# Sums of exponentials over edges of one source, as matmuls on a rounded part and a rest

## The chip, the cores and the metric

The kernel runs on one core of a Trainium2 chip. The metric is the device time of one execution in microseconds. Three runs of the kernel before gave a median of 1133.86 us (1133.8 to 1134.31).

## The reference

Four graph layers work in turn on a state of 16 batches, 512 nodes and 128 features: a diffusion layer, a graph attention layer ("gat"), an edge attention layer ("edge") and a Chebyshev layer with self-attention and a feed-forward part ("cheb", "att", "ffn"). The change lies in the edge layer alone. With E = 256 edges and 4 heads it is, per batch:

```
Qs = Xq[:, src];  Kt = Xq[:, dst]
e = einsum('behd,hd->beh', leaky_relu(Qs + Kt, 0.2), a)
e = e + log(A0[src, dst] + 1e-08)
m = segment_max(e_t, src)
ex = exp(e_t - m[src])
denom = segment_sum(ex, src)
attn = ex / denom[src]
Y = segment_sum(attn * Vt, src)
```

So each edge and head has an exponential, and these are summed over all edges with the same source. All is in f32.

## The kernel before

Every batch goes through the layers alone, and different batches are in different layers at the same time. A front part (up to about 410 us) computes the diffusion layer for all batches and, squeezed into it, the gat and edge layers of the first batches. Then each engine works through a list of steps, written out by hand. A fill list (FILL_ORDER) comes first, then ten rounds of one fixed list (ORDER), from 605 to 1037 us, then a drain list (DRAIN_ORDER). In a round the gat layer is at batch n, the edge layer at n - 1, the cheb layer at n - 2, attention at n - 3. A "+" behind a step's name in the list takes it from a batch further back. An engine does its steps strictly in the order of its list; between engines there are semaphores, which count, and `ready(engine, name, n, count, per)` waits until the semaphore has reached n x per + count.

Of the edge layer these steps matter here. Edges lie on the 128 partitions in ET = 2 groups; the small numbers of an edge (4 heads x 2 groups = 8 per partition) are rows of the tile edge_small.
- edge_le (VectorE, line 304): logit less the maximum.
- edge_exp (ScalarE, 263): the exponentials, into row 2 of edge_small.
- edge_den (TensorE, 374): the sums. The stationary matrix is a 128 x 128 block of same_src, which holds 1 where two edges have one source, and the moving part is the 4 exponentials of a group; 2 x 2 such matmuls, all in f32, go into the PSUM bank b0.
- edge_rden, edge_attn (VectorE, 309 and 313): the reciprocal of the sums, straight from b0, and the normalised weight.
- edge_u (VectorE, 318), edge_scatter (TensorE, 381): weighted values, and their sum over a node's edges.

In a round's list on VectorE the two attention masks att_mask12 and att_mask13 (line 2457) and the statistics n3_stats of the feed-forward part (line 2142) stand between edge_le and edge_rden. On TensorE edge_den follows edge_v (367), the values of an edge; behind edge_den come att_turn10 (2665), gat_pv0 (567), att_turn11 and edge_scatter.

Elsewhere in the kernel, tiles of the type float32r ("R32") hold rounded f32 numbers, and products that need more accuracy are done on a rounded part and a rest, as in `for i, part in enumerate([h2_hi, h2_lo])` of edge_gather.

Of the kernel before, what the change touches and what calls it, by code (L numbers as in the profile page):

```python
# [61 lines left out]
def build(nc, t_in, out):  # L62
    ctx = ExitStack()
    with ctx:
        def sb(name, shape, dt=F32, c=None):
# [42 lines left out]
        same_src = sb("same_src", [P, ET, E])  # L108
# [34 lines left out]
        k["pair_words"] = 3 * NT * N + 4 * NT * D + 3 * E + ET * H * E // 2 + 6 * ET * H + ET * D + (6 + 2 + 4) * NT  # L143
# [52 lines left out]


def edge_stage(nc, k, sem):
# [73 lines left out]
    def on_vector(dve):  # L272
# [306 lines left out]
def build_front(nc, k):  # L579
# [3 lines left out]
    with ExitStack() as c:  # L583
# [469 lines left out]
        def _(dve):  # L1053
# [255 lines left out]
            def segments():  # L1309
                dve.wait_ge(sem("rows"), 2 * ET)  # L1310
                nc.vector.tensor_scalar(k.seg_bias[:], k.same_src[:], BIG, -BIG, ALU.mult, ALU.add
                                        ).then_inc(sem("seg"), 1)
# [4 lines left out]

            def with_layers(lev, t):
# [49 lines left out]
                elif (lev, t) == (2, 1):  # L1368
                    for h in range(H):
                        edge[f"edge_max{h}"](0)  # L1370
                    edge["edge_le"](0)
# [4 lines left out]
                    gat["gat_row3"](1)
                elif (lev, t) == (2, 2):
                    gat["gat_max0"](1)
                    gat["gat_max1"](1)
# [452 lines left out]
    "edge": """  # L1832
        edge_lc
# [44 lines left out]
        cheb_qlow edge_max0 edge_max1 edge_max2 edge_max3 edge_le att_mask12 att_mask13 n3_stats+ edge_rden edge_attn  # L1878
# [50 lines left out]
        gat_stats:3 edge_rden:1 edge_attn:1 edge_u:1 gat_aggr:3 att_mask0:0 att_mask1:0 edge_x3:1 cheb_stats:1  # L1929
        cheb_aggr:1 gat_apply:3 gat_x2a:2 gat_x2b:2 att_mask2:0 edge_stats:2 att_mask3:0 edge_aggr:2 att_mask4:0  # L1930
        att_mask5:0 cheb_lo:1 gat_scores0:3 gat_scores1:3 gat_scores2:3 gat_scores3:3 gat_row1:3 att_mask6:0
        gat_max0:3 gat_max1:3 gat_row2:3 gat_max2:3 gat_row3:3 cheb_y:1 att_mask7:0 n1_stats:1 att_mask8:0 n1_aggr:1
        edge_z:2 n1_apply:1 att_mask9:0 cheb_x1:1 edge_lc:2 gat_max3:3 att_mask10:0 edge_max0:2 edge_max1:2
        edge_max2:2 edge_max3:2 cheb_qlow:1 edge_le:2 att_mask11:0 att_mask12:0 gat_rinv:3 att_mask13:0 edge_rden:2
        edge_attn:2 edge_u:2 att_mask14:0 cheb_klow:1 att_mask15:0 gat_stats:4 att_rv:0 edge_x3:2 gat_aggr:4
        att_mask0:1 cheb_stats:2 gat_x2a:3 cheb_aggr:2 att_mask1:1 gat_x2b:3 edge_stats:3 att_mask2:1 edge_aggr:3
        gat_apply:4 att_scale:0 cheb_lo:2 att_mask3:1 ffn_y2:0 n2_stats:0 n2_aggr:0 att_mask4:1 n2_apply:0 att_mask5:1
        att_mask6:1 gat_scores0:4 gat_scores1:4 gat_scores2:4 gat_scores3:4 gat_row1:4 cheb_y:2 gat_row2:4 n1_stats:2
        att_mask7:1 n1_aggr:2 gat_row3:4 ffn_y3:0 gat_max0:4 gat_max1:4 gat_max2:4 att_mask8:1 att_mask9:1 n1_apply:2
        edge_z:3 gat_max3:4 cheb_x1:2 edge_lc:3 att_mask10:1 att_mask11:1 edge_max0:3 edge_max1:3 edge_max2:3  # L1940
        gat_rinv:4 edge_max3:3 edge_le:3 att_mask12:1 gat_stats:5 cheb_qlow:2 edge_rden:3 edge_attn:3 edge_u:3
        att_mask13:1 n3_stats:0 n3_aggr:0 gat_aggr:5 cheb_klow:2 att_mask14:1 n3_apply:0 att_mask15:1 edge_x3:3
        cheb_stats:3 att_rv:1 gat_x2a:4 gat_x2b:4 cheb_aggr:3 edge_stats:4 gat_apply:5 att_mask0:2 att_mask1:2
        edge_aggr:4 cheb_lo:3 att_scale:1 att_mask2:2 att_mask3:2 ffn_y2:1 n2_stats:1 att_mask4:2 n2_aggr:1
        att_mask5:2 n2_apply:1 att_mask6:2 cheb_y:3 n1_stats:3 gat_scores0:5 gat_scores1:5 gat_scores2:5 gat_scores3:5
        gat_row1:5 att_mask7:2 gat_row2:5 n1_aggr:3 ffn_y3:1 gat_row3:5 gat_max0:5 att_mask8:2 n1_apply:3 att_mask9:2
        gat_max1:5 cheb_x1:3 gat_max2:5 gat_max3:5 edge_z:4 edge_lc:4 att_mask10:2 att_mask11:2 edge_max0:4
        cheb_qlow:3 edge_max1:4 edge_max2:4 edge_max3:4 edge_le:4 att_mask12:2 att_mask13:2 n3_stats:1 edge_rden:4
        edge_attn:4
# [67 lines left out]
        att_mask15:13 edge_rden:15 edge_attn:15 edge_u:15 att_rv:13 n3_apply:12 att_mask0:14 edge_x3:15 cheb_stats:15  # L2017
        cheb_aggr:15 att_mask1:14 att_mask2:14 att_scale:13 att_mask3:14 cheb_lo:15 ffn_y2:13 n2_stats:13 n2_aggr:13
        att_mask4:14 n2_apply:13 cheb_y:15 n1_stats:15 n1_aggr:15 n1_apply:15 cheb_x1:15 att_mask5:14 att_mask6:14
        att_mask7:14 cheb_qlow:15 att_mask8:14 att_mask9:14 cheb_klow:15 att_mask10:14 att_mask11:14 att_mask12:14  # L2020
        att_mask13:14 ffn_y3:13 att_mask14:14 n3_stats:13 att_mask15:14 att_rv:14 n3_aggr:13 att_mask0:15 n3_apply:13
        att_mask1:15 att_mask2:15 att_scale:14 att_copy1:15 att_mask3:15 att_mask4:15 att_mask5:15 ffn_y2:14
        att_copy3:15 att_mask6:15 att_mask7:15 att_mask8:15 n2_stats:14 att_rv_0:15 att_copy5:15 n2_aggr:14
        att_mask9:15 att_mask10:15 n2_apply:14 att_copy7:15 att_mask11:15 att_mask12:15 att_copy9:15 att_mask13:15
        att_copy11:15 att_scale_0:15 att_mask14:15 att_mask15:15 att_copy13:15 ffn_y3:14 n3_stats:14 att_rv_1:15
        n3_aggr:14 ffn_y2_0:15 n2_stats_0:15 n2_aggr_0:15 att_copy15:15 n2_gain_0:15 n2_apply_0:15 n3_apply:14
        att_scale_1:15 ffn_y2_1:15 n2_stats_1:15 n2_aggr_1:15 n2_gain_1:15 n2_apply_1:15 ffn_y3_0:15 n3_stats_0:15
        n3_aggr_0:15 n3_gain_0:15 n3_apply_0:15 ffn_final_0:15 ffn_y3_1:15 n3_stats_1:15 n3_aggr_1:15 n3_gain_1:15
        n3_apply_1:15 ffn_final_1:15
# [771 lines left out]
```

## Time and profile before

| | |
|---|---|
| median of three runs | 1133.86 us |
| the profiled execution | 1133.88 us |
| its span | 1132.0 us |
| TensorE busy | 1083.0 us, 96% |
| VectorE busy | 853.7 us, 75% |
| ScalarE busy | 757.9 us, 67% |
| GpSimd busy | 344.9 us, 30% |
| mean granted TensorE clock | 0.989 |

All times are of one execution, in microseconds from the span's start. PE is the matmul part of TensorE, PEld its loading of stationary matrices, DVE is VectorE, ACT ScalarE, POOL GpSimd and SP the engine that issues transfers. A matmul of plain f32 leaves two records on PE, and two on PEld. What stands in brackets behind a row is the engine's idle time before it and what ended it. The granted clock is a share of the full 2.4 GHz.

### The profile page before, as it was taken

The page shows a single profiled execution, that of the slowest core. Times are in us where ns is not written, and L with a number is a line of the kernel's source. Part 1 is how long each engine was busy: PE and PEld are TensorE (multiplying, and loading weights), DVE is VectorE, ACT ScalarE, POOL GpSimd, SP SyncE. Part 2 cuts the span into 40 slices and gives each one's busy share as a digit, 9 for nine tenths or more (in the row PEclk, how much of TensorE's full clock was granted, in tenths as well). Part 3 has the DMA queues.
Part 4 walks back from the last instruction along what each step waited for, and adds up shares of the span by engine and source line. Part 5 has one row for each costly group of instructions (what it writes and reads, how often), then busy time and mean ns, then how long its engine had stood idle before and what let it go on. Part 6 is the DMA issues. An engine that isn't in the chain of part 4 may idle for free. (4 is left out here: it accounts for less than half of the span.)

```text
span 1132.0 us, 21408 instructions
## 1 busy us (share of the span) xinstructions
PE 1083.0 (96%) x7105; PEld 866.6 (77%) x7105; DVE 853.7 (75%) x3073; ACT 757.9 (67%) x1640; POOL 344.9 (30%) x465
## 2 busy tenths in 40 slices
PE   8999999999999978999999999999999999999876
PEld 5679889889889866777777877778778778777554
DVE  7774434444435558898999999999999999988766
ACT  4444434433313235988988988988988989988864
POOL 3302002301241112143253253253252352333333
PEclk9999999998999999999999999999999999999999
DMA  3002030030330112342352352343343443432531
GB/s 96 19 10 57 10 94 10 10 94 10 85 99 1 29 38 77 102 131 76 94 140 78 101 137 77 106 124 87 106 116 86 111 115 85 120 107 61 142 94 28
DMA packets 132941, 89.42 MB, mean 79 GB/s; under 512 B 13664, under 2 KB 115424, under 8 KB 132832
## 3 DMA queue, kind: packets, MB, share of 16 engines
q1 hardware_dynamic: 132768, 88.07, 28.3%
q8 instruction: 56, 0.92, 0.3%
q14 instruction: 53, 0.43, 0.1%
q0 software_dynamic: 64, 0.00, 0.0%
HBM read 33.50 MB, written 20.97 MB: 48 GB/s over the span
## 5 line engine op out<-in xcount | busy, mean ns | idle before, releaser
L2360 ACT ACTIVATE att_Es<-att_Ts,att_small 128x512 f32<-128x512 f32 x256 | 184.9, 724 | 8.9 <-DVE att_small L2457 8.2
L2457 DVE CUSTOM_DVE_ANT_0 att_Ts<-bank,mask_att 128x512 f32<-128x512 f32 x256 | 172.0, 683 | 22.4 <-PE bank L2612 18.3
L2369 ACT COPY att_PTs<-bank 128x512 f32<-128x512 f32 x248 | 144.5, 583 | 51.9 <-PE bank L2665 51.1
L2665 PE MATMUL bank<-ident,att_Es 128*128 128x128 f32 x1024 | 155.8, 275 | 6.8 <-ACT att_PTs L2369 6.6
L2665 PEld LDWEIGHTS bank<-ident,att_Es 128*128 128x128 f32 x1024 | 121.3, 142 | 42.8 <-ACT att_PTs L2369 17.3
L2612 PE MATMUL bank<-K_parts,Q_parts 128*128 128x512 f32 x256 | 113.1, 471 | 5.5 <-DVE att_small L2457 3.9
L2154 POOL TENSOR_SCALAR n_rs<-n_mv 128x4 f32<-128x4 f32 x46 | 15.5, 338 | 282.4 <-DVE n_mv L2149 282.4
L1597 PE MATMUL bank<-G_hi,UT_parts 128*128 128x384 f32 x288 | 79.1, 345 | 1.8 <-DVE G_lo L1440 1.8
L567 PE MATMUL bank<-gat_whs,gat_ETs 128*128 128x128 f32 x512 | 63.7, 280 | 2.0 <-PEq L149 2.0
L784 POOL TENSOR_SCALAR l_rs<-l_mv 128x4 f32<-128x4 f32 x16 | 3.8, 236 | 198.6 <-DVE l_mv L1064 198.2
L2612 PEld LDWEIGHTS bank<-K_parts,Q_parts 128*128 128x128 f32 x256 | 45.5, 190 | 24.2 <-issue 13.5
L567 PEld LDWEIGHTS bank<-gat_whs,gat_ETs 128*128 128x128 f32 x512 | 61.2, 196 | 2.4 <-issue 2.2
L1597 PEld LDWEIGHTS bank<-G_hi,UT_parts 128*128 128x128 f32 x288 | 54.0, 193 | 2.8 <-issue 2.2
L2733 PE MATMUL bank<-att_PTs,v_in 128*32 128x512 f32 x480 | 54.9, 593 | 0.4 <-ACT att_PTs L2369 0.4
L450 ACT ACTIVATE gat_Ts<-gat_Vs,gat_small 128x512 f32<-128x512 f32 x64 | 46.1, 722 | 7.9 <-DVE gat_Vs L505 7.6
L1603 PE MATMUL bank<-Z_hi,P3T_hi 128*128 128x512 f32 x128 | 51.2, 400 | 0.0
L1073 DVE TENSOR_TENSOR UT_parts<-bank,UT_parts 128x512 fp32r<-128x512 f32 x36 | 24.4, 687 | 34.9 <-ACT UT_parts L884 34.7
L1603 PE MATMUL bank<-Z_hi,P3T_lo 128*128 128x512 f32 x128 | 50.2, 393 | 0.0
L2360 ACT ACTIVATION_READ_ACCUMULATOR att_Es<-att_Ts,att_small 128x1 f32 x256 | 50.1, 196 | 0.0
L1603 PE MATMUL bank<-Z_lo,P3T_hi 128*128 128x512 f32 x128 | 49.8, 389 | 0.0
L1597 PE MATMUL bank<-G_lo,UT_parts 128*128 128x384 f32 x144 | 49.4, 343 | 0.0
L2156 POOL TENSOR_TENSOR n_rs<-n_rs,neg_half 128x4 f32<-128x4 f32 x46 | 47.8, 1040 | 3.8
(350 smaller groups left out, 2904.0 us busy)
## 6 DMA issues: line engine op xcount, KB each, us to landing
Q_parts<-q_hi SPq DMA_DIRECT2D x128, 64.0 KB, 2.2
Q_parts<-q_lo SPq DMA_DIRECT2D x128, 64.0 KB, 2.0
K_parts<-k_hi SPq DMA_DIRECT2D x128, 64.0 KB, 2.0
K_parts<-k_lo SPq DMA_DIRECT2D x128, 64.0 KB, 2.0
l_x<-in_x SPq DMA_DIRECT2D x16, 256.0 KB, 2.8
gat_z<-x_after_l SPq DMA_DIRECT2D x16, 256.0 KB, 3.3
gat_xin<-x_after_l SPq DMA_DIRECT2D x16, 256.0 KB, 3.7
attn_residual<-cheb_x1s SPq DMA_DIRECT2D x16, 256.0 KB, 2.2
```

The costliest lines, as they stand in the source:

```text
L450: nc.scalar.activation(g.T[:, t, :], g.V[:, t, :], ACT.Exp, scale=0.8, bias=small[:, 4, t:t + 1], accum_out=small[:, 6, t:t + 1]).then_inc ...
L567: mm = nc.tensor.matmul(a0[:, cols(t)], g.ET[:, s, cols(t)], WhA[:, s, 0:D], start=(s == 0), stop=(s == NT - 1))
L1073: nc.vector.tensor_tensor(UT[:, b % 2, i, 1, :], bank[[6, 4, 5][i]][:], UT[:, b % 2, i, 0, :].bitcast(F32), ALU.subtract).then_inc(sem("ut ...
L1597: mm = nc.tensor.matmul(bank[t][:, 0:BLOCKS * D], left, right[:, i, :], start=(i == 0 and p == 0), stop=(i == BLOCKS - 1 and p == 2))
L1603: mm = nc.tensor.matmul(bank[t][:], left[:, s, cols(t)], right[:, s, :], start=(first and i == 0), stop=(stop and i == 2))
L2156: nc.gpsimd.tensor_tensor(rs[:, 1, :], rs[:, 0, :], k.neg_half[:], ALU.pow).then_inc(sem(tag + "_rs"), 1)
L2360: nc.scalar.activation(att_E[:, j % RING_E, :], att_T[:, j % RING_T, :], ACT.Exp, scale=-1.0, bias=att_small[:, 0, j:j + 1], accum_out=att ...
L2369: nc.scalar.copy(att_PT[:, h, :, cols(q)], c2[:].rearrange("p (s q) -> p s q", q=P)).then_inc(sem("att_pt"), 1)
L2457: nc.vector.tensor_tensor_reduce(att_T[:, j % RING_T, :], [c0, c1][j % 2][:], k.mask_att[:, tile_of(n, j)[1], :], -QK_SCALE, HUGE, ALU.add ...
L2612: return nc.tensor.matmul(dst, left, right, start=True, stop=True)
L2665: mm = nc.tensor.transpose(dst[:, cols(s)], att_E[:, i % RING_E, cols(s)], k.ident[:])
L2733: mm = nc.tensor.matmul(b0[r, :], vD[:, s, r], att_PT[:, h, s, :], start=(s == 0), stop=(s == NT - 1))
```

## The change

The exponentials are split on VectorE in a new step edge_exs: a copy into a float32r tile (edge_ex), which rounds, and a subtraction that leaves the rest, also in float32r. For each group of edges the 4 rounded numbers and the 4 rests lie side by side. same_src becomes float32r. The four matmuls of edge_den then each have 8 moving columns instead of 4, and both operands are float32r. The sums of the rounded parts and of the rests come out as two sets of columns in b0, so edge_rden first copies one set out, adds the other, and then takes the reciprocal. The semaphore edge_exp now counts three for each batch, one from ScalarE and two from VectorE, and edge_den waits for all three; edge_rden counts three as well.

In all lists of VectorE, edge_exs stands directly ahead of edge_rden; no other step has another place.

```
@@ -105 @@
-        same_src = sb("same_src", [P, ET, E])
+        same_src = sb("same_src", [P, ET, E], R32)
@@ edge_memory @@
+                   ex=sb("edge_ex", [P, ET, 2, H], R32),
@@ on_vector @@
+        def edge_exs(n):
+            ex = small[:, 2, :].rearrange("p (e h) -> p e h", h=H)
+            ready(dve, "edge_exp", n, 1, 3)
+            nc.vector.tensor_copy(g.ex[:, :, 0, :], ex).then_inc(sem("edge_exp"), 1)
+            ready(dve, "edge_exp", n, 2, 3)
+            nc.vector.tensor_tensor(g.ex[:, :, 1, :], ex, g.ex[:, :, 0, :].bitcast(F32), ALU.subtract
+                                    ).then_inc(sem("edge_exp"), 1)
+
         def edge_rden(n):
+            both = b0[:, 0:2 * ET * H].rearrange("p (e u h) -> p e u h", u=2, h=H)
+            total = small[:, 3, :].rearrange("p (e h) -> p e h", h=H)
             ready(dve, "edge_den", n)
-            nc.vector.reciprocal(small[:, 3, :], b0[:, 0:ET * H]).then_inc(sem("edge_rden"), 1)
+            nc.vector.tensor_copy(total, both[:, :, 0, :]).then_inc(sem("edge_rden"), 1)
+            ready(dve, "edge_rden", n, 1, 3)
+            nc.vector.tensor_tensor(total, both[:, :, 1, :], total, ALU.add).then_inc(sem("edge_rden"), 1)
+            ready(dve, "edge_rden", n, 2, 3)
+            nc.vector.reciprocal(small[:, 3, :], small[:, 3, :]).then_inc(sem("edge_rden"), 1)
@@ on_tensor @@
         def edge_den(n):
-            ready(pe, "edge_exp", n)
+            ready(pe, "edge_exp", n, 3, 3)
             for e in range(ET):
                 for f in range(ET):
-                    mm = nc.tensor.matmul(b0[:, e * H:e * H + H], k.same_src[:, f, cols(e)],
-                                          small[:, 2, f * H:f * H + H], start=(f == 0), stop=(f == ET - 1))
+                    mm = nc.tensor.matmul(b0[:, 2 * e * H:2 * (e + 1) * H], k.same_src[:, f, cols(e)],
+                                          g.ex[:, f, :, :].rearrange("p u h -> p (u h)"), start=(f == 0),
+                                          stop=(f == ET - 1))
@@ ORDER, DVE @@
-        cheb_qlow edge_max0 edge_max1 edge_max2 edge_max3 edge_le att_mask12 att_mask13 n3_stats+ edge_rden edge_attn
+        cheb_qlow edge_max0 edge_max1 edge_max2 edge_max3 edge_le att_mask12 att_mask13 n3_stats+ edge_exs edge_rden
+        edge_attn
...
```

VectorE in one of the rounds, before: the end of the masks, the statistics, the reciprocal of the sums, the weights and the weighted values.

```order
L2457 ISA att_Ts,att_small<-bank,mask_att 128x512
L2457 ISA att_small 128x1
L2142 BN_STATS n_stat<-ffn_y3s 128x6 x4
L309 RECIPROCAL edge_small<-bank 128x8
L313 TENSOR_TENSOR edge_small<-edge_small 128x8
L318 TENSOR_TENSOR edge_us<-bank,edge_small 128x256
```

And the same place now, from behind the statistics on (the line numbers are those of the changed kernel):

```order
L310 CAST edge_ex<-edge_small 128x2x4
L312 TENSOR_TENSOR edge_ex<-edge_small,edge_ex 128x2x4
L319 COPY edge_small<-bank 128x8
L321 TENSOR_TENSOR edge_small<-bank,edge_small 128x8
L323 RECIPROCAL edge_small<-edge_small 128x8
L327 TENSOR_TENSOR edge_small<-edge_small 128x8
L332 TENSOR_TENSOR edge_us<-bank,edge_small 128x256
```

The rounding copy and the subtraction have come in where the reciprocal stood, and the copy and the addition of the two sets of sums behind them.

TensorE in the same round, before: the values of an edge (L367), the sums (L374), two transposes of attention weights (L2665) around the gat layer's product, the scatter (L381).

```order
L2665 MATMUL bank<-ident,att_Es 128x128 x4
L367 MATMUL bank<-w_WvalT,edge_hgs 128x128 x2
L374 MATMUL bank<-edge_small,same_src 128x4 x4
L2665 MATMUL bank<-ident,att_Es 128x128 x4
L567 MATMUL bank<-gat_whs,gat_ETs 128x128 x8
L2665 MATMUL bank<-ident,att_Es 128x128 x4
L381 MATMUL bank<-src_rows,edge_us 128x512 x2
```

And now:

```order
L2683 MATMUL bank<-ident,att_Es 128x128 x4
L381 MATMUL bank<-w_WvalT,edge_hgs 128x128 x2
L388 MATMUL bank<-edge_ex,same_src 128x8 x4
L2683 MATMUL bank<-ident,att_Es 128x128 x4
L582 MATMUL bank<-gat_whs,gat_ETs 128x128 x8
L2683 MATMUL bank<-ident,att_Es 128x128 x4
L396 MATMUL bank<-src_rows,edge_us 128x512 x2
```

Nothing moved on TensorE; the four matmuls of the sums stand at the same place, with 8 columns from another tile.

## Rows read from the trace of the kernel before

**Rows 1.** The page, busy us of each engine, its share, its instructions
```profile
PE 1083.0 (96%) x7105; PEld 866.6 (77%) x7105; DVE 853.7 (75%) x3073; ACT 757.9 (67%) x1640; POOL 344.9 (30%) x465
```

**Rows 2.** Windows by stage: fill, one round; length, busy us, clock, DMA
```profile
380.00:605.00 225.00, 210.45 (x1468) 167.53 (x1467) 185.55 (x726) 163.73 (x376) 61.01 (x89) 0.98 0.32 87
...
777.67:820.84 43.17, 42.77 (x325) 33.71 (x323) 40.75 (x160) 38.52 (x89) 16.67 (x22) 1.00 0.38 106
```

**Rows 3.** Waits in one round: who, for whom, us in total, times, longest
```profile
...
PE bank L2602 <- DVE cheb_x1s L2445: 0.4, 1, 0.4
...
DVE att_Ts L2457 <- PE bank L2612: 0.6, 2, 0.3
...
```

**Rows 4.** Timeline in a round: start us, length us, engine, line, operation
```profile
777.80 0.24 ACT L263 ACTIVATE edge_small<-edge_small 128x8 f32<-128x8 f32 x1
...
778.09 0.97 PEld L374 LDWEIGHTS bank<-edge_small,same_src 128*128 128x128 f32 x8
...
779.64 0.19 DVE L309 RECIPROCAL edge_small<-bank 128x8 f32<-128x8 f32 x1
779.87 0.17 DVE L313 TENSOR_TENSOR edge_small<-edge_small 128x8 f32<-128x8 f32 x1
...
780.07 0.42 DVE L318 TENSOR_TENSOR edge_us<-bank,edge_small 128x256 f32<-128x256 f32 x1
```

**Rows 5.** Timeline, sums and reciprocal of batches 0 to 4 and 15
```profile
399.25 0.97 PEld L374 LDWEIGHTS bank<-edge_small,same_src 128*128 128x128 f32 x8
...
401.85 0.20 DVE L309 RECIPROCAL edge_small<-bank 128x8 f32<-128x8 f32 x1
...
439.00 0.97 PEld L374 LDWEIGHTS bank<-edge_small,same_src 128*128 128x128 f32 x8
...
440.10 0.21 DVE L309 RECIPROCAL edge_small<-bank 128x8 f32<-128x8 f32 x1
...
473.18 1.09 PEld L374 LDWEIGHTS bank<-edge_small,same_src 128*128 128x128 f32 x8 [0.24 <-issue]
...
474.39 0.21 DVE L309 RECIPROCAL edge_small<-bank 128x8 f32<-128x8 f32 x1
...
516.41 0.97 PEld L374 LDWEIGHTS bank<-edge_small,same_src 128*128 128x128 f32 x8
...
518.00 0.20 DVE L309 RECIPROCAL edge_small<-bank 128x8 f32<-128x8 f32 x1
...
562.52 0.97 PEld L374 LDWEIGHTS bank<-edge_small,same_src 128*128 128x128 f32 x8
...
563.90 0.19 DVE L309 RECIPROCAL edge_small<-bank 128x8 f32<-128x8 f32 x1
...
1037.89 0.97 PEld L374 LDWEIGHTS bank<-edge_small,same_src 128*128 128x128 f32 x8
...
1038.98 0.21 DVE L309 RECIPROCAL edge_small<-bank 128x8 f32<-128x8 f32 x1 [0.17 <-PE bank L374]
```

**Rows 6.** Timeline, VectorE, the last wait for TensorE in a round
```profile
796.01 0.69 DVE L2457 CUSTOM_DVE_ANT_0 att_Ts<-bank,mask_att 128x512 f32<-128x512 f32 x1 [0.32 <-PE bank L2612]
```

**Rows 7.** Waits of TensorE in the fill, 380 to 605 us
```profile
...
PE bank L2612 <- DMA K_parts<-k_lo: 1.1, 1, 1.1
...
```

**Rows 8.** Timeline, TensorE, the matmuls of one column
```profile
265.88 4.44 PE L1664 MATMUL bank<-vec,asym 128*128 128x1 f32 x32
```

**Rows 9.** Windows around low clocks; the granted clock is third from the end
```profile
...
269.00:275.00 6.00, 6.00 (x22) 6.00 (x22) 0.62 (x2) 0.00 (x0) 1.47 (x3) 0.50 0.00 0
408.00:411.00 3.00, 0.97 (x9) 0.76 (x8) 0.35 (x2) 1.07 (x2) 0.00 (x0) 1.00 0.00 0
411.00:416.00 5.00, 5.00 (x31) 4.89 (x30) 1.77 (x11) 1.97 (x5) 1.70 (x4) 0.66 0.19 56
1094.00:1097.00 3.00, 1.17 (x8) 0.81 (x8) 2.91 (x13) 1.99 (x5) 0.59 (x1) 1.00 0.77 228
1097.00:1102.00 5.00, 3.98 (x36) 2.59 (x36) 4.96 (x19) 3.41 (x8) 2.10 (x3) 1.00 0.08 24
...
```

More of the change, by code:

```diff
@@ L142, in build @@
         k["edge"] = pair_memory(nc, k.gat)
-        k["pair_words"] = 3 * NT * N + 4 * NT * D + 3 * E + ET * H * E // 2 + 6 * ET * H + ET * D + (6 + 2 + 4) * NT
+        k["pair_words"] = 3 * NT * N + 4 * NT * D + 3 * E + ET * H * E // 2 + 8 * ET * H + ET * D + (6 + 2 + 4) * NT
         k["gat_steps"] = gat_stage(nc, k, kept_sem)
@@ L191, in edge_memory @@
                    h2_lo=sb("h2_lo", [P, NT, D], R32), hg=sb("edge_hgs", [P, 2 * E]), xz=sb("edge_xzs", [P, E]),
-                   junk=sb("edge_junk", [P, ET * H, E], BF16), small=sb("edge_small", [P, 6, ET * H]),
+                   junk=sb("edge_junk", [P, ET * H, E], BF16), small=sb("edge_small", [P, 6, ET * H]), ex=sb("edge_ex", [P, ET, 2, H], R32),
                    U=sb("edge_us", [P, ET * D]), stat=sb("edge_stat", [P, NT, 6]), mv=sb("edge_mv", [P, NT, 2]),
@@ L328, in on_vector @@
         return ({"edge_stats": edge_stats, "edge_aggr": edge_aggr, "edge_z": edge_z, "edge_lc": edge_lc,
-                 "edge_le": edge_le, "edge_rden": edge_rden, "edge_attn": edge_attn, "edge_u": edge_u,
+                 "edge_le": edge_le, "edge_exs": edge_exs, "edge_rden": edge_rden, "edge_attn": edge_attn, "edge_u": edge_u,
                  "edge_x3": edge_x3} | {f"edge_max{h}": partial(edge_max, h=h) for h in range(H)})
@@ L1310, in segments @@
                 dve.wait_ge(sem("rows"), 2 * ET)
-                nc.vector.tensor_scalar(k.seg_bias[:], k.same_src[:], BIG, -BIG, ALU.mult, ALU.add
+                nc.vector.tensor_scalar(k.seg_bias[:], k.same_src[:].bitcast(F32), BIG, -BIG, ALU.mult, ALU.add
                                         ).then_inc(sem("seg"), 1)
@@ L1379, in with_layers @@
                     gat["gat_max1"](1)
+                    edge["edge_exs"](0)
                     edge["edge_rden"](0)
@@ L1832 @@
     "edge": """
+        edge_exs
         edge_lc
@@ L1928 @@
         cheb_qlow:0 gat_max3:2 edge_max0:1 edge_max1:1 edge_max2:1 edge_max3:1 edge_le:1 cheb_klow:0 gat_rinv:2
[L1929 to L1947, printed above, removed]
@@ L1948 @@
-        cheb_qlow:3 edge_max1:4 edge_max2:4 edge_max3:4 edge_le:4 att_mask12:2 att_mask13:2 n3_stats:1 edge_rden:4
-        edge_attn:4
+        gat_stats:3 edge_exs:1 edge_rden:1 edge_attn:1 edge_u:1 gat_aggr:3 att_mask0:0 att_mask1:0 edge_x3:1
+        cheb_stats:1 cheb_aggr:1 gat_apply:3 gat_x2a:2 gat_x2b:2 att_mask2:0 edge_stats:2 att_mask3:0 edge_aggr:2
+        att_mask4:0 att_mask5:0 cheb_lo:1 gat_scores0:3 gat_scores1:3 gat_scores2:3 gat_scores3:3 gat_row1:3
+        att_mask6:0 gat_max0:3 gat_max1:3 gat_row2:3 gat_max2:3 gat_row3:3 cheb_y:1 att_mask7:0 n1_stats:1 att_mask8:0
@@ new lines @@
+        n1_aggr:1 edge_z:2 n1_apply:1 att_mask9:0 cheb_x1:1 edge_lc:2 gat_max3:3 att_mask10:0 edge_max0:2 edge_max1:2
+        edge_max2:2 edge_max3:2 cheb_qlow:1 edge_le:2 att_mask11:0 att_mask12:0 gat_rinv:3 att_mask13:0 edge_exs:2
+        edge_rden:2 edge_attn:2 edge_u:2 att_mask14:0 cheb_klow:1 att_mask15:0 gat_stats:4 att_rv:0 edge_x3:2
+        gat_aggr:4 att_mask0:1 cheb_stats:2 gat_x2a:3 cheb_aggr:2 att_mask1:1 gat_x2b:3 edge_stats:3 att_mask2:1
+        edge_aggr:3 gat_apply:4 att_scale:0 cheb_lo:2 att_mask3:1 ffn_y2:0 n2_stats:0 n2_aggr:0 att_mask4:1 n2_apply:0
@@ new lines @@
+        att_mask5:1 att_mask6:1 gat_scores0:4 gat_scores1:4 gat_scores2:4 gat_scores3:4 gat_row1:4 cheb_y:2 gat_row2:4
+        n1_stats:2 att_mask7:1 n1_aggr:2 gat_row3:4 ffn_y3:0 gat_max0:4 gat_max1:4 gat_max2:4 att_mask8:1 att_mask9:1
+        n1_apply:2 edge_z:3 gat_max3:4 cheb_x1:2 edge_lc:3 att_mask10:1 att_mask11:1 edge_max0:3 edge_max1:3
+        edge_max2:3 gat_rinv:4 edge_max3:3 edge_le:3 att_mask12:1 gat_stats:5 cheb_qlow:2 edge_exs:3 edge_rden:3
+        edge_attn:3 edge_u:3 att_mask13:1 n3_stats:0 n3_aggr:0 gat_aggr:5 cheb_klow:2 att_mask14:1 n3_apply:0
@@ new lines @@
+        att_mask15:1 edge_x3:3 cheb_stats:3 att_rv:1 gat_x2a:4 gat_x2b:4 cheb_aggr:3 edge_stats:4 gat_apply:5
+        att_mask0:2 att_mask1:2 edge_aggr:4 cheb_lo:3 att_scale:1 att_mask2:2 att_mask3:2 ffn_y2:1 n2_stats:1
+        att_mask4:2 n2_aggr:1 att_mask5:2 n2_apply:1 att_mask6:2 cheb_y:3 n1_stats:3 gat_scores0:5 gat_scores1:5
+        gat_scores2:5 gat_scores3:5 gat_row1:5 att_mask7:2 gat_row2:5 n1_aggr:3 ffn_y3:1 gat_row3:5 gat_max0:5
+        att_mask8:2 n1_apply:3 att_mask9:2 gat_max1:5 cheb_x1:3 gat_max2:5 gat_max3:5 edge_z:4 edge_lc:4 att_mask10:2
@@ L1950 @@
+        att_mask11:2 edge_max0:4 cheb_qlow:3 edge_max1:4 edge_max2:4 edge_max3:4 edge_le:4 att_mask12:2 att_mask13:2
+        n3_stats:1 edge_exs:4 edge_rden:4 edge_attn:4
     """.split(),
@@ L2016 @@
         edge_lc:15 cheb_qlow:14 edge_max0:15 edge_max1:15 edge_max2:15 edge_max3:15 edge_le:15 cheb_klow:14 n3_aggr:12
[L2017 to L2029, printed above, removed]
+        att_mask15:13 edge_exs:15 edge_rden:15 edge_attn:15 edge_u:15 att_rv:13 n3_apply:12 att_mask0:14 edge_x3:15
+        cheb_stats:15 cheb_aggr:15 att_mask1:14 att_mask2:14 att_scale:13 att_mask3:14 cheb_lo:15 ffn_y2:13
@@ new lines @@
+        n2_stats:13 n2_aggr:13 att_mask4:14 n2_apply:13 cheb_y:15 n1_stats:15 n1_aggr:15 n1_apply:15 cheb_x1:15
+        att_mask5:14 att_mask6:14 att_mask7:14 cheb_qlow:15 att_mask8:14 att_mask9:14 cheb_klow:15 att_mask10:14
+        att_mask11:14 att_mask12:14 att_mask13:14 ffn_y3:13 att_mask14:14 n3_stats:13 att_mask15:14 att_rv:14
+        n3_aggr:13 att_mask0:15 n3_apply:13 att_mask1:15 att_mask2:15 att_scale:14 att_copy1:15 att_mask3:15
+        att_mask4:15 att_mask5:15 ffn_y2:14 att_copy3:15 att_mask6:15 att_mask7:15 att_mask8:15 n2_stats:14
@@ new lines @@
+        att_rv_0:15 att_copy5:15 n2_aggr:14 att_mask9:15 att_mask10:15 n2_apply:14 att_copy7:15 att_mask11:15
+        att_mask12:15 att_copy9:15 att_mask13:15 att_copy11:15 att_scale_0:15 att_mask14:15 att_mask15:15
+        att_copy13:15 ffn_y3:14 n3_stats:14 att_rv_1:15 n3_aggr:14 ffn_y2_0:15 n2_stats_0:15 n2_aggr_0:15
+        att_copy15:15 n2_gain_0:15 n2_apply_0:15 n3_apply:14 att_scale_1:15 ffn_y2_1:15 n2_stats_1:15 n2_aggr_1:15
+        n2_gain_1:15 n2_apply_1:15 ffn_y3_0:15 n3_stats_0:15 n3_aggr_0:15 n3_gain_0:15 n3_apply_0:15 ffn_final_0:15
@@ L2030 @@
+        ffn_y3_1:15 n3_stats_1:15 n3_aggr_1:15 n3_gain_1:15 n3_apply_1:15 ffn_final_1:15
     """.split(),
```

2 lines of the change are left out of this document (1 added, 1 removed).

## The prediction

> **What bounds the kernel now.** I read the busy shares first: TensorE (PE) 96%, VectorE (DVE) 75% of the span [rows 1]. A share over a span with several stages says little, so next came the busy time by stage: in the fill (380 to 605 us) PE works 210.45 of 225.00 us; then the rounds of the pipeline repeat every 43.17 us, with PE busy 42.77 and DVE 40.75 us [rows 2]. The waits of one such round leave PE one wait, 0.4 us on DVE, and DVE 0.6 us on PE's scores [rows 3]. So PE has no room in a round, and an idle microsecond put into its queue comes out as a later end, unless somebody catches up.
>
> Then the timeline around the changed step. In a round the exponentials end on ScalarE at 777.80 + 0.24 = 778.04, and PE starts the sums 0.05 us later, at 778.09, for 0.97 us. DVE at that moment has two masks and the statistics of another layer in front of it and comes to the reciprocal at 779.64 [rows 4]. Before the change that lateness costs nothing: the sums are long done. The change puts DVE work of this place between the exponentials and the sums, so what matters is, batch by batch, how far DVE's arrival R lies behind PE's start D.
>
> **The change part by part.**
>
> *The wait that is added.* The new step on DVE stands in the list directly ahead of the reciprocal, behind the masks and statistics, so its first instruction starts at the old R. It has two instructions, the second waiting for the first. Three dependent small instructions in a row start 0.23 and 0.20 us apart and the second lasts 0.17 us [rows 4]; I take 0.20 + 0.17, and 0.05 us to PE, together 0.42 us. PE then waits from D until R + 0.42. What stands behind the waiting sums in PE's queue (a transpose of attention weights, the product of the graph attention layer, another transpose, the scatter) waits too.
>
> *What is removed on PE.* Now four matmuls of plain f32 are eight records, 0.97 us, 0.121 us each. With rounded operands I expect one record each. No row shows a rounded matmul of 8 columns; the same weight tile costs 0.121 us per record now, so four give 0.49 us and 0.48 us is saved; the ends are no saving (0.97 us) and no time at all (0 us), which is +7.7 and -7.8 us over 16 batches. The value stays next to the measured row. The Trainium skill (TensorE: Matmul & The Clock Gate, section LDWEIGHTS) says that a weight load takes a time set by its number of columns alone, which by its formula is about 107 ns for 128; by this estimate four records take 0.43 us, 1 us less in all; the trace's 121 ns goes the same way.
>
> *PE's delay per batch* is therefore (R - D) + 0.42 - 0.48 = (R - D) - 0.06. From the pairs of rows [rows 5]: batch 0 has 401.85 - 399.25 = 2.60; batch 1 1.10; batch 2 1.21; batch 3 1.59; batch 4 1.38; batch 15 0.92 (DVE was free 0.17 us before its 1038.98). The ten batches 5 to 14 have 1.54 to 1.62, and 1.55 in the pair that is shown [rows 4]. Delays: 2.54 + 1.04 + 1.15 + 1.53 + 1.32 + 10 x 1.49 + 0.86 = 23.3 us.
>
> *What DVE adds.* The reciprocal now waits for sums that start at R + 0.42 and last 0.49; in batch 15, where DVE did wait, it started 1.09 us after the sums began, 0.12 us after their 0.97 [rows 5]. So it goes on at R + 1.03, then a copy, an addition and the reciprocal at 0.20, 0.20 and 0.23 us, and the normalised weights start at R + 1.66 where they start at R + 0.23 now: 1.43 us later. That is within 0.1 us of PE's 1.49 us, so neither hides the other and both engines move together.
>
> *Does it repeat in each round?* Follow the loop: PE from the end of the sums (779.06) to the score that DVE waits for at 796.01 [rows 6], 16.95 us, in PE's own order; then DVE from 796.01 to the next R, 779.64 + 43.17 = 822.81, 26.80 us with no wait on PE in it; then 0.42 and 0.49. That is 44.66 us against 43.17, again 1.49. The stall makes no slack that the next round can use, because DVE is held by PE at 796.01 and so comes equally late each time.
>
> *What is absorbed.* In the fill PE once waits 1.1 us for the transfer of keys [rows 7], in the round after batch 1; that transfer stands in a queue that issues one transfer after the other from before the sums on, so I let batch 1's 1.04 us vanish there: 22.3 us remain. In batch 0 the end of the front is passed on through the scatter and the output matmuls, so I keep its 2.54.
>
> *TensorE's clock.* The clock was granted in full in the rounds. It fell to the half level (1.2 of 2.4 GHz) during 4.44 us of matmuls of a single column [rows 8]; 269 to 275 read 0.50. It fell also after 408 to 411, where PE was busy 0.97 of 3 us: the five microseconds behind read 0.66. After 1094 to 1097, busy 1.17 of 3 us in pieces, it stayed at 1.00 [rows 9]. The change makes PE stand about 1.97 us per round and then run 0.49 us of 8-column matmuls: 2.5 us with almost nothing on the array, 3.5 us in batch 0. That is as near to the rows with a fall as to the one without, so some stalls will be followed by a fall and most not. A fall costs (1 - 0.66) x 5 = 1.7 us of full-speed work. I take three more falls than before, one in batch 0 and two later: 5.1 us; the ends are 0 and 16 falls, 0 and 27 us.
>
> *The rest* is nothing: the rounded tile of same-source flags holds the same zeros and ones, its bias is built from it once in the front, and the added memory of 16 words per partition moves no order.
>
> **Sum.** The profiled execution took 1133.88 us (span 1132.0 us and 1.9 us around it), against a median of 1133.86 us: the same. 1133.9 + 22.3 + 5.1 = 1161.3, so I say 1161 us.
>
> **Rivals.**
>
> *DVE catches up wholly, and the change is faster.* DVE has 43.17 - 40.75 = 2.4 us of idle time per round, more than the 1.97 us of the stall. If it came to the new step that much sooner against PE, the stall would be gone and the saving left: 16 x 0.48 = 7.7 us, 1126 us. The point from which it decides is R - D = 0.06 us, where stall and saving are equal. Against it: R - D is 0.9 us or more in all 16 batches, and the last stretch of 26.80 us ahead of R is worked off with no wait that a lead could fill. 3%.
>
> *DVE catches up in part.* If DVE's 0.6 us of waits on PE's scores in a round [rows 3] vanished, its own loop would be 43.17 - 0.6 + 1.43 = 44.0 us, 0.8 more than now: 10 x 0.8, and 7.4 us for the other batches less batch 1: about 1149 us. For it: PE would stand waiting and DVE would set the pace. Against it: the wait at 796.01 comes after PE work that starts when the sums end, so it should stay. 12%.
>
> *The clock falls after every stall.* 16 x 1.7 = 27 us on top of the 22.3 makes 1183 us. For it: the stall and the narrow matmuls lie together. Against it: the 1094 to 1097 row, and wide matmuls on both sides of a stall. 5%. The Trainium skill (TensorE: Matmul & The Clock Gate, section HAM oscillation) describes this very case, a clock that falls again in each round of a loop because of the idle gap in it; no row of the kernel before shows it in a round.
>
> **How the numbers follow.** The forecast, a stall of nearly the computed size in each batch and a few falls of the clock, has 80%. Its own range: without falls and with 2 us more absorbed 1154; with eight falls and batch 1 not absorbed 1133.9 + 23.3 + 13.6 = 1171. Towards the partial catch-up I go down to 1148, which also covers faster sums; the rest beyond both ends is under 2 in 10. Under 0.2% (2.3 us) is what a measurement here can't tell from no change. Faster 3% from the first rival; within 0.2% 2%, for a stall that only just pays for the saving; slower 95%.
>
> **What would show it.** PE's idle time should have a new large entry, the sums waiting for DVE's subtraction, near 2.0 us each in the rounds and 3.0 us in batch 0; the sums should be four records in about 0.5 us; DVE should show a wait of some 0.6 us for the sums ahead of the copy; the round should be 44.7 us, or some 46.4 us where the clock fell. I am wrong if the sums don't wait, if the round is 44.0 us or less (then DVE was not held by PE), if the sums still take near 1 us (rounding saves no pass), or if the clock falls in most rounds.

## Result and the profile after

The kernel after takes 1164.71 us (median of six runs, 1161.71 to 1170.49) against 1133.96 us of the kernel before beside it (six runs, 1128.59 to 1137.69): 1.028 times as long, interval 1.026 to 1.030, so 31 us slower. The prediction was 1161 us with a range of 1148 to 1171. The profiled execution of after took 1161.71 us, 27.8 us more than the one of before. One execution of the first experiment below took 1787.7 us at a mean clock of 0.567 and is left out of its ratio.

The busy shares of after, first lines of the page [rows 1 are those of before]:

```profile
span 1159.9 us, 21344 instructions
...
PE 1082.3 (93%) x7041; PEld 860.9 (74%) x7041; DVE 862.1 (74%) x3137; ACT 759.6 (65%) x1640; POOL 344.3 (30%) x465
```

PE does as much work as before in a span that is 27.9 us longer. It lost most of its time standing. The view of one line, the sums (now L388), says where: for each engine its records with the shortest, median and longest duration in ns, then what that engine waited for and who waited for it (us, times):

```profile
L388 PEld LDWEIGHTS bank<-edge_ex,same_src x64: 186/190/192, 400.2 to 1065.1; 128*128 128x128 f32 x64
...
its engine sat idle before it (us, times) until:
  DVE edge_ex L312: 57.1, 32
who waited for it (us, times):
  DVE edge_small L319: 11.2, 16
```

The 57.1 us count PE and PEld, 16 waits each. Of PEld alone they are 2.93 us in batch 0, then 1.59, 1.81, 1.92 and 1.75, nine times 1.91 or 1.92, and 1.88 and 1.24 at the end: 30.3 us. The records fell from 128 to 64. On VectorE the copy (L319) waits 0.70 us for the sums in each batch. Now the timeline around the sums, in a round (start, length, engine, line, operation, in brackets the idle time before) and in batch 0:

```profile
659.14 0.16 DVE L310 CAST edge_ex<-edge_small 128x8 fp32r<-128x8 f32 x1
659.33 0.17 DVE L312 TENSOR_TENSOR edge_ex<-edge_small,edge_ex 128x8 fp32r<-128x8 f32 x1
...
659.55 0.52 PEld L388 LDWEIGHTS bank<-edge_ex,same_src 128*128 128x128 f32 x4 [1.91 <-DVE edge_ex L312]
...
660.01 0.42 PEld L2683 LDWEIGHTS bank<-ident,att_Es 128*128 128x128 f32 x4
...
660.19 0.17 DVE L319 COPY edge_small<-bank 128x8 f32<-128x8 f32 x1 [0.70 <-PE bank L388]
...
660.59 0.20 DVE L323 RECIPROCAL edge_small<-edge_small 128x8 f32<-128x8 f32 x1
...
660.83 0.17 DVE L327 TENSOR_TENSOR edge_small<-edge_small 128x8 f32<-128x8 f32 x1
...
400.16 0.52 PEld L388 LDWEIGHTS bank<-edge_ex,same_src 128*128 128x128 f32 x4 [2.93 <-DVE edge_ex L312]
```

The sums start 0.41 us after VectorE comes to the split, last 0.52 us instead of the 0.97 of [rows 4], and the normalised weights start 1.69 us after the split. Now the windows, by time: length, busy us of PE, PEld, DVE, ACT and POOL, granted clock, DMA share and GB/s. First one round, then the whole stretch from the sums of batch 1 to those of batch 15, then the surroundings of one stall:

```profile
614.48:659.14 44.66, 42.53 (x318) 33.33 (x318) 41.44 (x164) 38.70 (x89) 16.62 (x22) 1.00 0.37 102
...
440.06:1064.82 624.76, 590.01 (x4320) 460.15 (x4321) 561.75 (x2199) 532.39 (x1211) 220.06 (x296) 0.99 0.36 99
...
702.00:704.60 2.60, 0.88 (x9) 0.69 (x7) 2.50 (x12) 2.60 (x7) 0.00 (x0) 1.00 0.12 28
704.60:705.90 1.30, 1.30 (x12) 1.30 (x13) 0.56 (x4) 0.28 (x3) 0.00 (x0) 1.00 0.00 0
705.90:709.30 3.40, 3.40 (x19) 3.40 (x18) 2.53 (x13) 1.85 (x5) 1.27 (x2) 0.51 0.12 28
```

The round is 44.66 us against 43.17 [rows 2]. The stretch from batch 1 to batch 15 took 598.89 us before (439.00 to 1037.89) and 624.76 after, so 25.9 of the 27.9 us arise in it. Behind the stall that ended at 704.59 the clock read 0.51, that is the lower level of 1.2 GHz, for 3.4 us. What that costs is seen in the windows of the graph attention product (L582) alone, in a round without a fall and in this one (length; PE and PEld busy; clock, DMA share, GB/s):

```profile
660.00:664.00 4.00, 1.95 (x16) 1.86 (x16) 1.00 0.07 16
705.00:709.50 4.50, 3.26 (x16) 3.07 (x16) 0.62 0.13 31
```

The same 16 matmuls take 3.26 us instead of 1.95. Rounds with a fall last 46.28 and 46.49 us, 1.6 and 1.8 us more than 44.66.

The sum by these rows: the waits less the shorter sums are 30.3 - 16 x 0.45 = 23.1 us. The clock can be estimated in the gross: a span times (1 - mean clock) is what it takes from a PE that always works; for before 1132.0 x 0.011 = 12.5 us, for after, with

```profile
core 0: 1159.9 us, clock 0.985
```

1159.9 x 0.015 = 17.4 us, 4.9 us more. 23.1 + 4.9 = 28.0 us, and 27.9 were measured between the two spans.

That this comes out so closely is in part luck. The mean clock has three digits, which leaves half a microsecond to either side, and it counts time in which PE has nothing to do: behind 1156 us the clock reads 0.50 and PE has no matmul left. By place, from the starts of the sums of each batch in both traces, the difference is made up otherwise. Three falls that before doesn't have, at 521.6, 705.9 and 931.2 us, add 1.7, 1.7 and 1.8 us, 5.2 together. Against them the part ahead of batch 1 came out shorter. PE arrived at the sums of batch 0 at 400.16 - 2.93 = 397.23 us instead of 399.25, 2.0 us sooner, though nothing is changed ahead of them. From there to the sums of batch 1 it took 1.0 us less than the waits and the saving give. On both ways the clock of the kernel before fell where that of after did not: it reads 0.50 at 269 to 275 us [rows 9], and 0.66 in the last of the windows here, of which the first two are those of after:

```profile
268.00:275.00 7.00, 7.00 (x50) 7.00 (x50) 2.88 (x13) 1.91 (x5) 1.69 (x4) 1.00 0.00 0
428.00:433.00 5.00, 4.33 (x16) 2.44 (x16) 5.00 (x17) 1.49 (x3) 0.22 (x1) 1.00 0.29 86
...
428.00:433.00 5.00, 5.00 (x16) 3.29 (x16) 4.25 (x13) 1.58 (x3) 0.00 (x0) 0.66 0.35 105
```

23.1 + 5.2 - 2.0 - 1.0 = 25.3 us. Of the 2.6 us that remain, 1.1 lie between the sums of batches 4 and 5 (0.7 of it a new wait of PE for VectorE at L353) and 1.4 behind the sums of batch 15, where PE's last matmuls ran at the lower clock; the rest cancels.

### The profile page after: what moved, and what is told of

Read it like the earlier page. It is cut to its first block and busy times, and to the rows that moved or that the text cites. A ratio compares the mean times of both kernels' runs of the same rounds, so it can differ in the third digit from the quotient of the medians.

```text
span 1159.9 us, 21344 instructions
## 1 busy us (share of the span) xinstructions
PE 1082.3 (93%) x7041; PEld 860.9 (74%) x7041; DVE 862.1 (74%) x3137; ACT 759.6 (65%) x1640; POOL 344.3 (30%) x465
## 3 DMA queue, kind: packets, MB, share of 16 engines
q1 hardware_dynamic: 132768, 88.07, 27.8%
## 5 line engine op out<-in xcount | busy, mean ns | idle before, releaser
L2683 PEld LDWEIGHTS bank<-ident,att_Es 128*128 128x128 f32 x1024 | 121.2, 142 | 43.0 <-ACT att_PTs L2387 17.4
L582 PE MATMUL bank<-gat_whs,gat_ETs 128*128 128x128 f32 x512 | 66.0, 286 | 2.0 <-PEq L149 2.0
L582 PEld LDWEIGHTS bank<-gat_whs,gat_ETs 128*128 128x128 f32 x512 | 63.3, 202 | 2.4 <-issue 2.2
```

Of the source, the lines that this page charges most:

```text
L582: mm = nc.tensor.matmul(a0[:, cols(t)], g.ET[:, s, cols(t)], WhA[:, s, 0:D], start=(s == 0), stop=(s == NT - 1))
L2683: mm = nc.tensor.transpose(dst[:, cols(s)], att_E[:, i % RING_E, cols(s)], k.ident[:])
```

## Experiments

The theory: VectorE's place in its list makes PE wait, the wait repeats in each round, and the waits make the clock fall now and then. The first rival: VectorE's own added work makes the round longer. The second: the new matmuls cost more than they save. Three kernels take one part each, a fourth shortens the wait.

**VectorE's work without the wait.** PE takes the sums as before; VectorE does all its new work on the side.

```
-            ready(pe, "edge_exp", n, 3, 3)
+            ready(pe, "edge_exp", n, 1, 3)
...
+                    mm = nc.tensor.matmul(b0[:, e * H:e * H + H], k.same_src[:, f, cols(e)],
+                                          small[:, 2, f * H:f * H + H], start=(f == 0), stop=(f == ET - 1))
...
+            nc.vector.tensor_tensor(total, both, total, ALU.max).then_inc(sem("edge_rden"), 1)
```

> VectorE does all its new work at the new places (split, copy, combination, reciprocal), but the sums run in plain f32 from the unsplit exponentials as before and wait for ScalarE alone; the split numbers are used by nobody, and the combination takes a maximum of the same sums. Theory S (TensorE stands at the sums until VectorE has split): no stall, so 1134 us, give or take 4. Theory V (VectorE, busy 94% of a round, has become the bound by its four added instructions): about as long as the changed kernel, 1160 to 1166 us.

Measured: 1136.48 us, ratio 1.002 (0.999 to 1.005). Its window of one round, and its timeline at the sums:

```profile
689.84:733.03 43.19, 42.79 (x324) 33.72 (x324) 41.24 (x163) 38.49 (x89) 16.65 (x22) 1.00 0.38 105
```

```profile
776.18 0.97 PEld L388 LDWEIGHTS bank<-edge_small,same_src 128*128 128x128 f32 x8
...
777.74 0.15 DVE L310 CAST edge_ex<-edge_small 128x8 fp32r<-128x8 f32 x1
777.92 0.17 DVE L312 TENSOR_TENSOR edge_ex<-edge_small,edge_ex 128x8 fp32r<-128x8 f32 x1
778.01 0.16 DVE L319 COPY edge_small<-bank 128x8 f32<-128x8 f32 x1
```

VectorE does its four extra instructions, none of the rows waits, and the round grows by 0.02 us. The first rival is out: VectorE has room for the work. It lacks room only at this place.

**The wait with plain f32.** The kernel after, with same_src and edge_ex in plain f32.

```
-        same_src = sb("same_src", [P, ET, E], R32)
+        same_src = sb("same_src", [P, ET, E])
...
-                   ... ex=sb("edge_ex", [P, ET, 2, H], R32),
+                   ... ex=sb("edge_ex", [P, ET, 2, H]),
```

> The changed kernel with plain f32 in place of the rounded type for the flags and the split numbers (the rest is then zero). The wait stays, the saved passes come back. Theory S: eight records in the sums again, 0.97 us for 0.52, so 16 x 0.45 = 7 us more than the changed kernel's 1165: 1172 us. If the rounded type saves nothing that reaches the end (VectorE is the bound): the same as the changed kernel, 1165 us.

Measured: 1179.81 us, ratio 1.042 (1.037 to 1.046). The line of the sums, the sums in a timeline, and a window of a round:

```profile
L388 PEld LDWEIGHTS bank<-edge_ex,same_src x128: 186/192/338, 397.7 to 1077.5; 128*128 128x128 f32 x128
...
  DVE edge_ex L312: 57.1, 32
```

```profile
756.22 0.97 PEld L388 LDWEIGHTS bank<-edge_ex,same_src 128*128 128x128 f32 x8 [1.91 <-DVE edge_ex L312]
```

```profile
801.31:846.39 45.08, 42.95 (x322) 33.75 (x322) 41.43 (x162) 38.70 (x90) 16.65 (x22) 1.00 0.37 100
```

The wait is the same 57.1 us, the records are 128 again, and the round is 0.42 us longer than after's. So the rounded form saves what it was thought to save, and the second rival is out. That is 6.7 us over 16 batches. The other 8 us to the kernel after go with a lower clock, 0.975 in the profiled execution against 0.985, and four of its ten rounds hold a fall instead of two; they were not separated further.

**The rounding without the wait.** The kernel before, where ScalarE writes rounded exponentials at once; there is no split, and the rests are left out.

```
-            nc.scalar.activation(small[:, 2, :], small[:, 1, :], ACT.Exp)
+            nc.scalar.activation(g.ex[:], small[:, 1, :], ACT.Exp)
...
-                                          small[:, 2, f * H:f * H + H], start=(f == 0), stop=(f == ET - 1))
+                                          g.ex[:, f * H:f * H + H], start=(f == 0), stop=(f == ET - 1))
```

> The kernel before with rounded operands alone: ScalarE writes the exponentials rounded, nothing is split, the rest is left out of sums and weights; VectorE's lists are those of before. Theory S: the saving by itself, 16 x 0.45 = 7 us, 1127 us. A rival that holds the saving for hidden: 1134 us.

Measured: 1128.37 us, ratio 0.995 (0.993 to 0.998). Its window of a round, its timeline on PEld, and a row of its waits (us, times, longest):

```profile
773.00:815.85 42.85, 42.44 (x321) 33.31 (x319) 40.70 (x159) 38.52 (x89) 16.62 (x22) 1.00 0.39 106
```

```profile
773.00 0.52 PEld L374 LDWEIGHTS bank<-edge_ex,same_src 128*128 128x128 f32 x4
773.48 0.42 PEld L2665 LDWEIGHTS bank<-ident,att_Es 128*128 128x128 f32 x4
```

```profile
PEld bank L2665 <- ACT att_PTs L2369: 0.9, 3, 0.4
```

The sums are as short as after's, but only 0.32 us per round arrive of the 0.45. The transposes behind them (L2665) wait in three places of the round for ScalarE's copy out of their bank, 0.9 us; in the kernel before it is two places and 0.7 us. That was a note at the time; it came back below.

**The split two steps earlier.** Only VectorE's lists are changed: edge_exs goes behind the mask that follows edge_le, with one mask and the statistics after it.

```
-        ... edge_le att_mask12 att_mask13 n3_stats+ edge_exs edge_rden
+        ... edge_le att_mask12 edge_exs att_mask13 n3_stats+ edge_rden
```

> The changed kernel with the split placed one step behind the logits (in the rounds behind the first of the two masks) instead of ahead of the reciprocal; the same instructions. Theory S: R lies 0.15 us behind the old start of the sums, the stall shrinks from 1.91 to about 0.6 us and the saving of 0.45 nearly pays for it: 0.1 us a round, 1134 to 1138 us. Theory V: VectorE has as much work as in the changed kernel, so 1160 us or more.

Measured: 1136.11 us, ratio 1.003 (1.000 to 1.006). The timeline of a round:

```profile
784.24 0.17 DVE L310 CAST edge_ex<-edge_small 128x8 fp32r<-128x8 f32 x1
...
784.44 0.17 DVE L312 TENSOR_TENSOR edge_ex<-edge_small,edge_ex 128x8 fp32r<-128x8 f32 x1
...
784.66 0.52 PEld L388 LDWEIGHTS bank<-edge_ex,same_src 128*128 128x128 f32 x4 [0.53 <-DVE edge_ex L312]
```

The place alone takes the ratio from 1.028 to 1.003, some 28 us. With a wait of 0.53 and a saving of 0.45 the round should be 43.25 us, and most rounds are 43.27 to 43.29. One takes 44.73 us at a clock of 1.00; single longer rounds of this kind stand in other traces too (43.82 us before, 45.04 after), and their cause was not looked for.

**The stall filled.** What do the falls of the clock cost? The kernel after again, and beside it the same kernel with two matmuls of 512 columns per batch ahead of the wait; their numbers are overwritten.

```
+            for _ in range(2):
+                nc.tensor.matmul(b0[:], k.ident[:], k.src_rows[:, 0, :], start=True, stop=True)
             ready(pe, "edge_exp", n, 3, 3)
```

> The changed kernel itself, on the chip of the next two runs: 1165 us, with one run or another 4 us to either side, as in its first six. In the runs with the lower mean clock the time is longer.

> The changed kernel with two matmuls of 512 columns in plain f32 put ahead of the wait of the sums, whose results the sums write over. They take 4 x 0.43 = 1.72 us of TensorE, less than the 1.91 us stall of a round. Theory S with the clock: they cost nothing in the rounds, TensorE's wait shrinks to about 0.2 us, and the clock no longer falls there; two to four falls of 1.7 us go: 1159 to 1162 us. A rival by which the stall is not idle time at all (TensorE held up by its own work): 16 x 1.72 = 27 us more, 1192 us. A rival by which the falls have nothing to do with the stall: 1165 us.

Measured: 1169.04 us for the first (six runs, 1159.75 to 1170.2; ratio 1.028, 1.025 to 1.032) and 1157.24 us for the second (ratio 1.020, 1.017 to 1.023). The span and mean clock of the first, then the same row, the windows of the stretch from batch 1 to batch 15 and of a round, and the timeline of the second:

```profile
core 0: 1168.1 us, clock 0.978
```

```profile
core 0: 1158.2 us, clock 0.988
```

```profile
443.42:1063.19 619.77, 607.70 (x4377) 465.38 (x4377) 561.57 (x2199) 532.30 (x1211) 220.19 (x296) 1.00 0.37 100
...
794.44:839.11 44.67, 44.26 (x323) 33.96 (x323) 41.44 (x162) 38.72 (x90) 16.62 (x22) 1.00 0.37 101
```

```profile
792.45 0.30 PEld L386 LDWEIGHTS bank<-src_rows,ident 128*128 128x128 f32 x2
792.56 1.88 PE L386 MATMUL bank<-src_rows,ident 128*128 128x512 f32 x4
...
794.22 0.17 DVE L312 TENSOR_TENSOR edge_ex<-edge_small,edge_ex 128x8 fp32r<-128x8 f32 x1
...
794.44 0.52 PEld L390 LDWEIGHTS bank<-edge_ex,same_src 128*128 128x128 f32 x4 [0.83 <-DVE edge_ex L312]
```

The round is as long as after's: 1.88 us of useless work fit into the stall at no cost, and the sums still start 0.22 us behind VectorE's subtraction. PEld's wait is 0.83 us and not the 0.2 expected, since the loads of the fillers are done long before their matmuls. But the clock reads 1.00 from the sums of batch 1 to those of batch 15, and the kernel is 11.8 us faster than the unfilled one on the same chip, more than was expected.

Not all of the 11.8 us is the price of the new stalls. Between 405 and 450 us the kernel before has falls too (0.66 at 411 to 416 us [rows 9] and at 428 to 433), and the filled kernel has none there. The clean comparison is the stretch from batch 1 to batch 15, where before reads 1.00 as well: 619.77 us filled, and unfilled 624.76 us with three falls in the first profiled execution and 626.75 (445.10 to 1071.85) with four in the second. All seven falls begin 1.3 to 2.0 us behind the end of a stall. So the falls behind the stalls cost some 5.0 and 7.0 us.

The two profiled executions of the unfilled kernel differ by the clock: by the gross estimate the second lost 1168.1 x 0.022 = 25.7 us to it, 8.3 more than the first, and it took 1169.90 us, 8.2 more than 1161.71. But 3.4 of the 8.2 us were lost ahead of the first sums, which start at 403.55 us instead of 400.16, where nothing is changed; and the six runs of the kernel before lie 9 us apart too (1128.59 to 1137.69). The spread of about 10 us is one of the clock, but not of the stalls alone.

**The sums moved as well.** The version with the shorter wait, and edge_den one step later on PE, behind the first of the transposes.

```
-        ... att_turn9 edge_v edge_den att_turn10 gat_pv0 att_turn11 edge_scatter
+        ... att_turn9 edge_v att_turn10 edge_den gat_pv0 att_turn11 edge_scatter
```

> The split one step behind the logits on VectorE, as in the run before with that edit, and the sums one step later on TensorE, behind a transpose of attention weights that takes 0.45 us. Theory S: the wait of 0.53 us that was left there shrinks to 0.1 us, the saving stays: a round of 42.8 to 43.0 us, 1128 to 1131 us. If VectorE's added work is by now the bound: no better than with the split alone moved, 1136 us.

Measured: 1140.82 us, ratio 1.006 (1.003 to 1.008): a miss by 10 us. The sums wait no more, in any batch, and yet most rounds stay at 43.24 to 43.26 us. I took this for VectorE's loop, now the bound with 43.24 us, and took VectorE's work down to test it.

**Less work on VectorE.** The shorter wait; ScalarE writes the rounded exponentials with a second Exp, VectorE only subtracts, and one reduction takes the place of copy and addition. The second kernel has the sums moved on top.

```
-            nc.vector.tensor_copy(g.ex[:, :, 0, :], ex).then_inc(sem("edge_exp"), 1)
+            nc.scalar.activation(g.ex[:, :, 0, :], small[:, 1, :].rearrange(...), ACT.Exp)
...
+            nc.vector.tensor_reduce(total, both, AX, ALU.add).then_inc(sem("edge_rden"), 1)
```

> The split one step behind the logits, and two of the four added VectorE instructions gone: ScalarE writes the rounded exponentials itself (a second exponential, 0.24 us), VectorE only subtracts; the two sets of sums are added by one reduction. Theory now: with the stall nearly gone VectorE's own loop is the bound, 43.24 us a round with four added instructions and 42.85 with none. So TensorE's loop sets the end here: a stall of 0.3 to 0.4 us less the saving of 0.45, a round of 43.1 us, 1133 to 1136 us. If VectorE's work is no bound at all: no better than 1136 us.

> The same with the sums one step later on TensorE. No stall is left; VectorE has two added instructions and gets 0.35 to 0.4 us of its loop back: a round of 42.85 to 43.0 us against 43.24 with four, 4 us less in all than the run with both moved: 1135 to 1137 us, below 1134 only if the fill lists don't pay for the moved sums. If VectorE is not the bound: 43.24 us again and 1141 us.

Measured: 1133.88 us without the move, ratio 0.9995 (0.997 to 1.002), and 1140.03 us with it, 1.005 (1.003 to 1.007): the second is a miss again. Its round is 43.25 us as before, though VectorE has less to do; so VectorE's loop wasn't the bound and that theory falls. The timelines show what is. First without the move, then with it:

```profile
776.66 0.61 ACT L2392 COPY att_PTs<-bank 128x512 f32<-128x512 f32 x1
...
777.10 0.52 PEld L386 LDWEIGHTS bank<-edge_ex,same_src 128*128 128x128 f32 x4 [0.31 <-DVE edge_ex L312]
...
777.57 0.42 PEld L2688 LDWEIGHTS bank<-ident,att_Es 128*128 128x128 f32 x4
...
777.96 0.75 PEld L580 LDWEIGHTS bank<-gat_whs,gat_ETs 128*128 128x128 f32 x6
```

```profile
777.80 0.61 ACT L2397 COPY att_PTs<-bank 128x512 f32<-128x512 f32 x1
...
778.45 0.42 PEld L2693 LDWEIGHTS bank<-ident,att_Es 128*128 128x128 f32 x4 [0.51 <-ACT att_PTs L2397]
...
778.84 0.53 PEld L386 LDWEIGHTS bank<-edge_ex,same_src 128*128 128x128 f32 x4
...
779.29 1.31 PEld L580 LDWEIGHTS bank<-gat_whs,gat_ETs 128*128 128x128 f32 x11
```

The transposes need the bank that ScalarE empties with the copy. The copy ends at 777.27 in the first, while PE is at the sums, and hides behind them. In the second the transposes come to it first and stand 0.51 us, until the copy ends at 778.41; the sums follow. From the start of the copy to the product (L580) it is 1.30 us in the first and 1.49 in the second, 0.19 more, and the rounds are 43.06 and 43.25 us. The move exchanged a wait of 0.31 us for one of 0.51. It is the same wait that kept 0.13 us per round of the plain rounding. That the copy is the bound is only read from these two traces; no kernel with a much earlier copy was run. In the run before these, without the second Exp, the copy starts 0.08 us sooner behind the first Exp and the transposes wait 0.42 us, and still the round is the same, which the reading doesn't explain. Nor do the rounds account for all of the loss: from the sums of batch 5 to those of batch 15 the two kernels take 431.79 and 434.13 us, 2.3 us apart, and their medians are 6.2 us apart. The rest lies in the fill and drain lists, in which the sums were moved too, and was not broken down.

No version that keeps the rests beats the kernel before.

## Why the prediction was right

The order on VectorE, the wait it makes and its repetition in every round were as written; most steps hold to some hundredths, and two were off. That the profiled execution is within 1 us of the forecast owes something to luck, since falls of the clock that before had and after had not took back 3 us there.

- The wait from R and D: 1.91 us in the rounds and 2.93 in batch 0, for about 2.0 and 3.0. Without the wait, VectorE's work costs nothing; with the place moved, the 28 us go.
- The sums: 64 records instead of 128, and 0.45 us saved instead of 0.48. Eight records take 0.97 us and four 0.52, so each record that went saved 0.11 us and not the average of 0.121. Sum of the delays 23.1 us, for 23.3; the wait and the saving were both taken a little too large, which cancels in part.
- Round 44.66 us, as worked out, and VectorE held 0.70 us at the sums, for some 0.6. The rivals in which VectorE catches up are out: its waits at PE's scores, on which both engines shift together, stayed at 0.6 us in a round, and so did the stall, 1.91 us in the first round and 1.88 in the tenth.
- Off: "I let batch 1's 1.04 us vanish". The delay was paid in full. From batch 1 to batch 2 the kernel takes 35.57 us for 34.18, 1.39 more, which is what batch 2's own wait costs (1.81 - 0.45); nothing was given back there. PE's wait for the scores of that stretch is as long as before, 1.1 us [rows 7]; the profile now puts it down to VectorE's mask and not to the transfer:

```profile
451.44 0.48 PE L2630 MATMUL bank<-K_parts,Q_parts 128*128 128x512 f32 x1 [1.10 <-DVE att_small L2475]
```

- Off: "one in batch 0 and two later", the clock. The three new falls of the profiled execution came at 521.6, 705.9 and 931.2 us and no new one in batch 0, where both kernels have a fall at 412 us [rows 9]. Nor is a row with a fall a rule: the 32 matmuls of one column of [rows 8] took 3.63 us in after, and the clock stayed at 1.00 behind them, at 268 to 275 us.
- "5.1 us" for the falls: 5.0 and 7.0 us in the two profiled executions, by the stretch from batch 1 to batch 15 against the filled kernel. The size was right; what the clock takes outside this stretch, ahead of the first sums and at the end, was not in the prediction and differs from run to run. The medians leave 7.7 us (1164.71) and 10.9 us (1169.04) beyond 23.1 us over the medians of before beside them. Of the 3.4 us between the sum of 1161.3 and 1164.7, 0.8 us are the delays that were not absorbed (23.1 for 22.3); the other 2.6 us are left to the clock as a remainder.
- The rival of a fall behind each stall is out: 2 of the 10 rounds in one profiled execution, 3 of 10 in the other. The Trainium skill (TensorE: Matmul & The Clock Gate, section HAM oscillation) describes a loop that throttles again in each pass because of its idle gap; the trace agrees that gaps in a loop do it, but here 1.9 us of it did so only sometimes.

## What to carry to other kernels

Before an instruction of another engine is put between a producer and its consumer, look up when that engine's list comes to the place: 0.37 us of work cost 1.9 us each time, and two list places earlier it cost almost nothing. A stall on TensorE may cost a second time through the clock, and that share differs from run to run; wide matmuls in the gap told the two apart here. When a wait is removed and the round stays, look at who waits next in the same queue before blaming the engine that did the waiting.

## What the hardware showed unexpectedly

- Stalls of the same 1.91 us, each followed by 0.5 us of 8-column matmuls, were followed by a fall of the clock in some rounds and not in others of one execution: 0.51 at 705.9 to 709.3 us, and 1.00 in the round from 614.48 to 659.14.
- Two 512-column f32 matmuls (1.88 us of PE time) in each stall cost no time in the round, and the clock read 1.00 from batch 1 to batch 15. Whether the gap or the narrow matmuls behind it bring the fall was not separated.
- The same 32 matmuls of one column stood ahead of a fall in one kernel's execution (0.50 at 269 to 275 us before [rows 9]) and of none in the other's (1.00 at 268 to 275 us after).
- A rounded matmul of 8 columns is one record where plain f32 is two: four take 0.52 us and eight 0.97. The number of columns made no difference at this size: eight records of plain f32 take 0.97 us with 8 columns (the second experiment) as with 4 [rows 4].
